# Two attention blocks and a feed-forward block on one core: self-attention's last batch with its side products in other slots

## What is computed

```python
x = _layernorm(tgt, ln1_g, ln1_b)
q, k, v = (_heads(t) for t in jnp.split(x @ sa_wqkv, 3, axis=-1))
wei = softmax(causal(einsum('bhtd,bhsd->bhts', q, k) * scale))
result = tgt + _merge(einsum('bhts,bhsd->bhtd', wei, v)) @ sa_wproj + sa_bproj
xq, xs = _layernorm(result, ln2_g, ln2_b), _layernorm(src, ln2_g, ln2_b)
k2, v2 = (_heads(t) for t in jnp.split(xs @ ed_wkv, 2, axis=-1))
q2 = _heads(xq @ ed_wq)
result = result + _merge(softmax(q2 @ k2 * scale) @ v2) @ ed_wproj + ed_bproj
result = result + relu(_layernorm(tgt, ln3_g, ln3_b) @ ff_w1 + ff_b1) @ ff_w2 + ff_b2
```

## Time and profile before

| | us |
|---|---|
| runs of the kernel, median of 3 | 1372.56 |
| lowest and highest run | 1371.2, 1374.21 |
| the profiled execution: span from first to last instruction | 1372.2 |
| PE busy in it | 1310.9 |
| POOL, VectorE, ScalarE busy | 701.5, 794.4, 662.1 |

### The profile page before, as it was taken

The page is one execution under the profiler, slowest core; times in us unless marked ns, Lnnn a source line. Parts: engine busy times, 40 slices in busy tenths (PEclk is TensorE's granted clock), DMA queues, the critical chain, the costliest instruction groups (busy, mean ns, idle before and its releaser), DMA issues.

```text
span 1372.2 us, 24578 instructions
## 1 busy us (share of the span) xinstructions
PE 1310.9 (96%) x9193; PEld 1082.5 (79%) x9193; DVE 794.4 (58%) x2007; ACT 662.1 (48%) x1609; POOL 701.5 (51%) x577
## 2 busy tenths in 40 slices
PE   7999999999899999998788999999999999999997
PEld 6888888888788888887677787878877787887874
DVE  6613223232777777776655575756757566575565
ACT  5311111232666665666433656474665647456444
POOL 3232221322444555556733767666676766667661
PEclk9999999999999999999599999999999999999999
DMA  7400102114647776547267685777677587766641
GB/s 237 145 18 16 62 31 77 46 60 117 139 86 178 166 186 148 122 123 185 63 142 119 100 128 98 132 123 125 101 127 120 101 137 104 142 101 112 90 71 41
DMA packets 100400, 151.67 MB, mean 111 GB/s; under 512 B 10197, under 2 KB 63229, under 8 KB 99514
## 3 DMA queue, kind: packets, MB, share of 16 engines
q1 hardware_dynamic: 100282, 150.11, 53.8%
HBM read 66.74 MB, written 24.12 MB: 66 GB/s over the span
## 4 chain that ended last, share of the span: by engine, by line
PE 76%; POOL 8%; issue 5%; DVE 5%; DMA 3%; ACT 2%; SPq 1%; POOLq 0%; ACTq 0%; DVEq 0%
PE ps L1727 18%; PE ps L453 11%; PE ps L164 10%; PE ps L423 10%; PE ps_pair L1744 6%; PE ps L1759 5%; PE ps L1773 5%; PE ps L1832 3%; POOL ca_partial L1586 2%; DMA ca_k_stack<-ca_keys 2%; POOL ca_xT L1473 1%; DMA sa_K_stack<-sa_rows 1%; PE ps L1207 1%; PE ps L1791 1%; PE ps L1227 1%
## 5 line engine op out<-in xcount | busy, mean ns | idle before, releaser
L1664 DVE TENSOR_REDUCE ca_maxes<-ps 112x1 f32<-112x375 f32 x512 | 256.5, 541 | 106.0 <-PE ps L1759 103.9
L1607 ACT ACTIVATE ca_probT<-ps_pair 125x448 f32<-125x448 f32 x384 | 210.3, 554 | 181.5 <-PE ps_pair L1744 179.6
L1586 POOL TENSOR_TENSOR ca_partial<-ca_partial,ca_probT 125x896 f32<-125x896 f32 x118 | 249.2, 2112 | 93.6 <-ACT ca_probT L1607 89.0
L312 POOL TENSOR_TENSOR ff_hT<-ff_hrelu,ff_hT 128x512 fp32r<-128x512 f32 (+1 forms) x64 | 77.9, 1218 | 203.2 <-DVE ff_hT L394 203.2
L1759 PE MATMUL ps<-ca_k_stack,ca_q_stack 96*112 96x376 f32 x512 | 168.7, 352 | 6.9 <-issue 3.6
L1744 PEld LDWEIGHTS ps_pair<-ca_q_stack,ca_k_stack 98*125 98x125 f32 x768 | 130.2, 186 | 44.0 <-issue 31.9
L1744 PE MATMUL ps_pair<-ca_q_stack,ca_k_stack 98*125 98x224 f32 x768 | 156.2, 285 | 1.3 <-ACT ca_probT L1607 1.2
L423 PE MATMUL ps<-ff_w,ff_hT 128*128 128x512 f32 x672 | 155.5, 390 | 0.0
L1727 PE MATMUL ps<-w_b,ca_xT 128*125 128x512 f32 x576 | 151.2, 398 | 3.1 <-POOL ca_xT L1473 2.5
L1727 PE MATMUL ps<-ca_xT,w_a 128*128 128x376 f32 x768 | 153.1, 335 | 0.0
L423 PEld LDWEIGHTS ps<-ff_w,ff_hT 128*128 128x128 f32 x672 | 125.6, 188 | 25.8
...
## 6 DMA issues: line engine op xcount, KB each, us to landing
...
```

Source lines behind the costliest of these rows:

```text
L312: pool.tensor_tensor(hT[:, LO, m % RING, 0:width(g)], hrelu[i % 2][:, 0:width(g)], hT[:, HI, m % RING, 0:width(g)].bitcast(F32), ALU.subtr ...
L1586: pool.tensor_tensor(total, total, half(a), ALU.add).then_inc(partial_done, 1)
L1607: act.activation(probT[u // GH][0:JT, u % GH].rearrange("p a t -> p (a t)"), ps_p[u % 2][0:JT, 0:2 * T], ACT.Exp).then_inc(exp_done, 1)
L1664: dve.tensor_reduce(maxes[:, q, j, a:a + 1], ps_s[n % 3][0:TQ, 0:JH], AX_X, ALU.max).then_inc(s_read, 1)
```

## The change

A third table, `FINAL_FILLS`, takes the place of `FILLS` in the last batch alone (slots 112 to 127). Against `FILLS` it has Y 5.2 in slot 117 (before 113), Y 5.3 in 122 (116), P 6.0 in 118 (117), P 6.1 in 120 (119), R 6.0 in 126 (124), R 6.1 in 127 (125), and no Y in slot 127: Y 6.0 goes to slot 128, and Y 6.1, Y 6.2 and Y 6.3 one slot later each, to 129, 130 and 131. The values' fills stay where they were. The two `normalise` items of batch 6 go from slots 122 and 123 to 124 and 125, and with them `store` to 125. For group 28 of the heads, `scale_hi` and `scale_lo` stand one slot later. Nothing is computed otherwise, and no instruction is added or taken away.

```diff
--- before.py
+++ after.py
@@ -675,7 +675,9 @@
 FILLS = {0: [("Y", -2, 1)], 1: [("Y", -2, 2)], 2: [("V", 0, 0)], 3: [("V", 0, 1)], 4: [("Y", -2, 3)], 5: [("P", -1, 0)],
          6: [("Q", 1, 0)], 7: [("P", -1, 1)], 8: [("K", 1, 0)], 9: [("Q", 1, 1)], 10: [("K", 1, 1)], 11: [("Q", 1, 2)],
          12: [("K", 1, 2), ("R", -1, 0)], 13: [("Q", 1, 3), ("R", -1, 1)], 14: [("K", 1, 3)], 15: [("Y", -1, 0)]}
-LAST_FILLS = {0: [("Y", -2, 1)], 1: [("Y", -2, 2)], 2: [("Y", -2, 3)], 4: [("P", -1, 0)], 5: [("P", -1, 1)],
+FINAL_FILLS = {0: [("Y", -2, 1)], 2: [("V", 0, 0)], 3: [("V", 0, 1)], 5: [("Y", -2, 2)], 6: [("P", -1, 0)], 8: [("P", -1, 1)],
+               10: [("Y", -2, 3)], 14: [("R", -1, 0)], 15: [("R", -1, 1)]}
+LAST_FILLS = {0: [("Y", -2, 0)], 1: [("Y", -2, 1)], 2: [("Y", -2, 2)], 3: [("Y", -2, 3)], 4: [("P", -1, 0)], 5: [("P", -1, 1)],
               10: [("R", -1, 0), ("R", -1, 1)], 12: [("Y", -1, 0)], 13: [("Y", -1, 1)], 14: [("Y", -1, 2), ("Y", -1, 3)]}
 Y_WEIGHTS = [3, 5]
 OUTPUT_WEIGHTS = [28, 44]
@@ -697,6 +699,9 @@
         if (name, m) == ("Y", 3):
             rest.append(("store_queries", b))
         return read, rest
+
+    def fills_of(b):
+        return FILLS if b < B - 1 else FINAL_FILLS if b == B - 1 else LAST_FILLS
 
     slots = 16 * B + 16
     NEXT_STATISTICS = {16 * (B - 1) + i: t for i, t in NEXT_MEASURED.items()}
@@ -729,14 +734,15 @@
             items.append(("value", G))
             reads[n + 1].append(("sums_read", G))
             rests[n + 1].append(("scale", G))
-            reads[n + 2].append(("scale_hi", G))
-            rests[n + 2].append(("scale_lo", G))
+            behind = 3 if G == 4 * (B - 1) else 2
+            reads[n + behind].append(("scale_hi", G))
+            rests[n + behind].append(("scale_lo", G))
         if b >= B - 1:
             items.append(("other_stage", n - 16 * B, BEFORE))
         if n < 4:
             fill = FIRST_FILLS[n]
         else:
-            fill = [(name, b + d, m) for name, d, m in (FILLS[i] if b < B else LAST_FILLS.get(i, []))
+            fill = [(name, b + d, m) for name, d, m in fills_of(b).get(i, [])
                     if 0 <= b + d < B and not (name == "V" and b == 0)]
         for name, c, m in fill:
             items.append((name, c, m))
@@ -751,9 +757,9 @@
                 items.append(("load_columns", b + 2))
             if i == 14:
                 items.append(("masks", b + 1))
-        normalised = (10, 11) if b < B else (9, 9)
+        normalised = (10, 11) if b < B - 1 else (12, 13) if b < B else (9, 9)
         items += [("normalise", b - 1, t) for t in range(2) if i == normalised[t] and 0 <= b - 1 < B]
-        if i == 11 and 0 <= b - 1 < B:
+        if i == normalised[1] and 0 <= b - 1 < B:
             items.append(("store", b - 1))
         if n in Y_WEIGHTS:
             u = Y_WEIGHTS.index(n)
```

## The result

| | before | changed |
|---|---|---|
| median of the runs | 1372.03 | 1382.24 |
| lowest and highest | 1371.2, 1374.21 | 1381.37, 1383.44 |
| span of the profiled execution | 1372.2 | 1380.5 |
| PE busy in it | 1310.9 | 1311.8 |

The ratio is 1.0077, with a 95% interval of 1.0065 to 1.0089: 10.2 us slower. The forecast had the sign and the main mechanism, but only 5.5 us, and 1382.24 lies above its range.

What follows compares the result with a forecast made beforehand. PE was taken to bound the kernel, so only its idle or slow time counts. The first T 2.4 later, 7.0 for R behind T, less 3.9 for a saved round: 5.5 us slower, 1378.1, range 1370.5 to 1381.

Steps and rivals of the forecast that it cites:

- the first T later: First context transpose on PE, put at 668.4, 2.35 us later, through P 6.0, its clock, VectorE and POOL.
- P 6.0's start: PE waits for scores, transposes and the product with the values ahead of P 6.0: start 642.1, 2.0 us later.
- The clock at P 6.0: A wait of about 3 us drops PE to 1.2 GHz for most of P 6.0: 1.8 us more.
- VectorE and POOL up to T: P's first addition 4.1 us later, 3.0 returned on VectorE; Y 5.3's split adds 1.25 on POOL's chain.
- R behind T: ScalarE reads R behind T's reads, so Y 6.0 starts 8.5 us behind T: 7.0 more, the largest term.
- Y to P 7.0: One round fewer between Y 6.0 and P 7.0 on PE: 19.1 instead of 22.98 us, returning 3.9.
- What P 7.0 loses, the end loses: Behind P 7.0 both kernels do the same work in the same order, so its delay passes to the end.
- VectorE is held up by POOL: Rival: the split of R 6.1 waits for POOL's normalised tile, 1.7 us more, 1379.8; chance 0.12.
- The clock stays up: Rival: later P and Y pieces keep PE at 2.4 GHz past 652, -0.9 us, 1371.7; chance 0.25.

Runs made afterwards that it cites:

- the repetition: The changed kernel, unedited, profiled once more: span 1381.9 us.
- the rounding later: The changed kernel with ScalarE's rounding of the third and fourth weight half one slot later: 1378.11 us, ratio 1.0051.
- R alone: The kernel before with only the change's part on R (normalise, R 6.0, R 6.1 and Y 6.0 onwards later): 1376.47 us, ratio 1.0038.
- the normalisation early: The changed kernel with normalise of batch 6 and its store back in slots 122 and 123: 1383.51 us, ratio 1.0085.
- L48 behind the split: The changed kernel with POOL's subtraction for the weight halves placed behind the split of Y 5.2: 1385.39 us, ratio 1.0098.
- the fills alone: The changed kernel with its part on R undone, so only Y 5.2, Y 5.3, P 6.0 and P 6.1 later: 1377.71 us, ratio 1.0045.

## Why the prediction was right in sign and wrong in size

The forecast was 5.5 us, all of it at P 7.0. Measured against the prediction's own execution, P 7.0 came 7.0 later; in the means of the executions it is 8.5, with 1.6 more behind P 7.0. Step by step, forecast and means of four executions of before and two of the changed kernel:

| step | forecast | one execution | means |
|---|---|---|---|
| the first T later | 2.35 | 3.1 | 3.2 |
| Y 6.0 behind T, more than before | 7.0 | 7.3 | 7.3 |
| Y 6.0 to P 7.0, less than before | 3.9 | 3.5 | 2.05 |
| behind P 7.0, later | 0 | 1.3 | 1.6 |

- **P 6.0's start** (put at 642.1, came at 643.82) is the first step that failed. 642.1 was 3.9 behind the rounding's start of 638.18; measured were 6.06 to 6.07 in six executions. Two things were missing. VectorE's L1144 stands still while POOL is in L48: without that the distance is 5.10 and 4.61. The sum counted POOL's splits of Y 5.2 and Y 5.3 only where they now stand, and not what their leaving lets POOL do: `keep_next` starts at once behind the rounding, 0.24 us ahead of L1144, where the split had held it back until 0.18 behind. The trace of before had the effect already: its copy L1126 took 1.46 us and ended 0.15 behind an L48 of POOL (0.30 at 649.42), and the normalisation at 654.18, whose 1.13 the prediction takes as its own length, stood beside POOL's L1029 until 655.02; the next one took 0.54. VectorE and POOL of before:

```profile
637.15 1.46 DVE L1126 COPY sa_rinv<-sa_inv 112x256 f32<-112x256 f32 x1
...
639.54 0.47 DVE L1138 TENSOR_TENSOR sa_oT<-sa_of,sa_oT 128x224 fp32r<-128x224 f32 x1 [0.93 <-ACT sa_oT L1051]
...
635.55 2.91 POOL L48 TENSOR_TENSOR w_a<-ctx_tokens,w_a 128x1024 fp32r<-128x1024 f32 x1
...
639.72 2.55 POOL L48 TENSOR_TENSOR w_b<-ctx_tokens,w_b 128x1024 fp32r<-128x1024 f32 x1
```

  The other is that the half clock begins ahead of P, at the transposes of 640.46 (0.81 us instead of 0.50) and in the product (1.35 instead of 0.78).
- **The clock at P 6.0**: 1.8 us were put in, 1.34 came in the profile (4.34 less 3.00), 1.83 in the repetition; with the rounding later P 6.0 was back at 3.03. Right in size, against a before at full clock. The claim that a wait of 2.06 ahead of P "did not make it fall" was true of the profiled execution and of one repetition; in the two others P 6.0 took 4.57.
- **VectorE and POOL up to T**: the first addition came 1.6 behind P's end, as put, and T at 669.18 instead of 668.4, since P 6.0 ended 1.4 later than put. The split of Y 5.3 on POOL's chain cost 0.94 instead of 1.25.
- **R behind T**: 8.5 was forecast, 8.75 measured, and 8.7 with R alone. Right.
- **Y to P 7.0**: 19.1 forecast, 19.52 measured, 20.07 in the repetition. What failed here is the number it was set against, and in the means this is the largest miss at P 7.0. The 22.98 of before has its rounds at half clock; in two of the four executions of before P 6.0 ran mostly at half clock, T came 1.3 to 2.4 later, and the pieces behind Y 6.0 ran at full clock (1.60 each), so that Y 6.0 to P 7.0 took 20.65 and 20.77. The whole stretch was as long as in the other two, but a round less is worth less there.
- **"What P 7.0 loses, the end loses"** held only to 1.6 us, and whether these belong to the change is open: in the changed kernel with the normalisation early, with L48 behind the split and with Y 5.3 in 121, P 7.0 to the end took 680.6 to 680.8, as little as in any execution of before. What the two profiled executions show is this. ScalarE's cast of keys waits for the DMA into the K stack, and with it a score of cross-attention, which starts at 731.00 before and at 737.99 now, the 7.0 of P 7.0 later; but before, the clock's next fall (720.3 to 723.7) lay ahead of this gate, where 1.5 us of idle time took it in, and in the changed kernel it came just behind it, where two half pieces of K took 1.55 and 2.08 instead of 1.20 and 1.19:

Before, and then changed:

```profile
731.00 0.40 PE L1759 MATMUL ps<-ca_k_stack,ca_q_stack 96*112 96x376 f32 x1 [1.50 <-issue]
...
731.23 1.20 PE L1727 MATMUL ps<-ca_xT,w_a 128*128 128x376 f32 x6
```

```profile
736.56 0.47 ACT L1646 CAST ca_keys<-ps 128x376 fp32r<-128x376 f32 x1 [4.85 <-DMA ca_k_stack<-ca_keys]
...
737.99 0.40 PE L1765 MATMUL ps<-ca_k_stack,ca_q_stack 96*112 96x376 f32 x1 [2.96 <-issue]
...
739.89 2.08 PE L1733 MATMUL ps<-ca_xT,w_a 128*128 128x376 f32 x6
```

- **The rivals**: that VectorE is held up by POOL had 0.12, and named the wrong operation. POOL's normalised tiles (L105) do not hold it: L1144 took 0.38 at 662.23 beside one, and the cast of R 6.1, the one the rival was about, 0.39 at 676.74 beside the sixth. (The tile that the rival calls the fifth is the sixth: by its own numbers the fifth ends 667.91 + 2.5 + 2.2 - 666.03 = 6.6 behind T.) POOL's operations with two operands, L48, L1021 and L1029, do. "The clock stays up" failed, though there was something in it: with the fills alone Y 6.1 and the pieces behind it ran at full clock (1.60 each), a round sooner than in the changed kernel.
- **The range** was too narrow because its bounds held each term's own uncertainty, and no bound for an engine that the layout had idle, and none for what one execution differs from the next. The 0.36 us between the span and the median compare two scales: a run's time is 1.8 to 3.1 us longer than the span of the same execution (1383.44 and 1380.5 in the changed kernel). The forecast adds a difference to both, so this did it no harm.
